# Count items' one-hots by one comparison with a scalar per partition and item, in place of packed two-tensor comparisons over six items

## The reference, cut to what matters

```python
xl = (x @ W_l + b_l); xr = (x @ W_r + b_r); e = edge_attr @ W_e
g = leaky_relu(xl[src] + xr[dst] + e, 0.2)
logits = einsum('ehc,hc->eh', g, att)
alpha = softmax of logits over the edges of each dst
out = segment_sum(xl[src] * alpha[..., None], dst)
```

## Time and profile before

| | |
|---|---|
| median of 3 runs | 7927.81 us (7926.12 to 7949.97) |
| the profiled execution: time, span | 7968.06, 7966.3 us |
| TensorE busy, share of the span | 5155.2 us, 65% |
| GpSimd busy | 3868.2 us, 49% |
| VectorE busy | 3099.9 us, 39% |
| ScalarE busy | 1675.7 us, 21% |
| mean granted TensorE clock | 0.736 |

### The profile page before, as it was taken

The page is one execution under the profiler, slowest core; times in us unless marked ns, Lnnn a source line. Parts: engine busy times, 40 slices in busy tenths (PEclk is TensorE's granted clock), DMA queues, the critical chain, the costliest instruction groups (busy, mean ns, idle before and its releaser), DMA issues. The chain is left out here.

```text
span 7966.3 us, 113832 instructions
## 1 busy us (share of the span) xinstructions
PE 5155.2 (65%) x33329; PEld 4083.2 (51%) x33329; DVE 3099.9 (39%) x3830; ACT 1675.7 (21%) x3525; POOL 3868.2 (49%) x3496
## 2 busy tenths in 40 slices
PE   0106888888888884166598895666666666614656
PEld 0103555555555553166355555666666666614656
DVE  3427777777777774444301103111111111122101
ACT  0004455455545542034000000111111111100000
POOL 0246888888888886200000003777777777640000
PEclk9958889888888886577798895555555555557988
DMA  6114555555555553299597792444444444405665
GB/s 278 33 38 134 146 150 153 145 152 144 150 146 149 148 150 83 66 368 360 141 292 230 233 296 70 127 124 127 124 127 124 127 124 127 114 20 186 233 234 194
DMA packets 597834, 1268.50 MB, mean 159 GB/s; under 512 B 201373, under 2 KB 367006, under 8 KB 572008
## 3 DMA queue, kind: packets, MB, share of 16 engines
q1 hardware_dynamic: 319400, 734.86, 29.0%
q10 hardware_dynamic: 166656, 412.78, 15.1%
q0 software_dynamic: 111424, 117.64, 8.4%
HBM read 930.29 MB, written 491.91 MB: 179 GB/s over the span
## 5 line engine op out<-in xcount | busy, mean ns | idle before, releaser
L513 POOL DMA_INDIRECT att_gl<-tab_l,att_ix x1568 | 1960.6, 1250 | 487.4 <-issue 461.0
L944 POOL DMA_INDIRECT sum_gl<-tab_l,sum_ixs x1568 | 1554.3, 991 | 541.3 <-issue 499.6
L753 ACT ACTIVATE att_acc<-att_pc 128x392 bf16<-128x392 f32 x2352 | 1084.9, 496 | 1334.3 <-PE att_pc L532 1188.5
L909 PE MATMUL sum_pm<-sum_msg,sum_S 128*128 128x64 f32 x3136 | 717.2, 423 | 661.7 <-ACT sum_msg L921 661.7
L529 PE MATMUL att_pc<-att_ohl,att_ohv 128*128 128x392 bf16 x2352 | 856.0, 364 | 290.1 <-DVE att_ohl L628 290.0
L909 PEld LDWEIGHTS sum_pm<-sum_msg,sum_S 128*128 128x128 f32 x3136 | 683.5, 330 | 689.4 <-issue 679.5
L532 PE MATMUL att_pc<-att_acc,att_ohv 128*128 128x392 bf16 x2352 | 848.5, 361 | 163.5 <-ACT att_acc L753 159.7
L1620 PE MATMUL l_pn<-l_a,l_E 128*128 128x392 bf16 x4704 | 792.5, 332 | 78.2 <-DVE l_E L1533 68.8
L216 POOL MEMSET tab_hT<- 1x6272 f32 x2 | 10.6, 5318 | 1643.2 <-POOLq L206 1643.2
L886 DVE TENSOR_TENSOR sum_t<-sum_pb,sum_gl 128x512 f32<-128x512 f32 x196 | 135.5, 691 | 1699.9 <-DMA sum_gl<-tab_l,sum_ixs 1699.9
L897 PE MATMUL sum_pb<-sum_wbs,sum_ea 64*128 64x64 f32 x3136 | 694.5, 419 | 21.5 <-DMA sum_ea<-in_ea64T 21.5
(11 more groups left out here) (301 smaller groups left out, 5418.2 us busy)
## 6 DMA issues: line engine op xcount, KB each, us to landing
A<-att_acc SPq DMA_DIRECT2D x2352, 98.0 KB
l_a<-A SPq DMA_DIRECT2D x294, 784.0 KB, 4.3
l_at<-AT SPq DMA_DIRECT2D x98, 1568.0 KB
att_dall<-in_dst ACTq DMA_DIRECT2D x224, 448.0 KB
sum_dall<-in_dst SPq DMA_DIRECT2D x196, 512.0 KB, 5.0
tr_a<-A SPq DMA_DIRECT2D x49, 1568.0 KB, 11.7
AT<-tr_at ACTq DMA_DIRECT2D x49, 1568.0 KB, 12.0
tot<-att_o ACTq DMA_DIRECT2D x56, 1022.0 KB
```

What stands on the lines that cost most here:

```text
L513: nc.gpsimd.indirect_dma_start(out=gl[s][:, c, :], out_offset=None, in_=g.tab_l, in_offset=bass.IndirectOffsetOnAxis(ap=ix[s][:, c:c + 1], ...
L753: nc.scalar.activation(acc[c][m][:, :], pc[c][m % 2][:, 0:LO], ACT.Copy).then_inc(s_acc[c], 1)
L909: mm = nc.tensor.matmul(pm[s][:, j // SB, (j % SB) * W:(j % SB + 1) * W], S[s][:, j, :], msg[s][:, j, :], start=True, stop=True)
L944: nc.gpsimd.indirect_dma_start(out=gl[s][:, j, :], out_offset=None, in_=g.tab_l, in_offset=bass.IndirectOffsetOnAxis(ap=ixs[s][:, j:j + 1] ...
```

## The change

`items` makes, for each of the six items by itself, three tensor_scalar comparisons: the constant row of 128 numbers with rk, the same row with the kept flag, and the constant row of 392 with lo. The scalar is one 4-byte value per partition, taken from a column of `g.rk`, `g.keep` or `g.lo`. The doubled constants are single now, and the one-hots are stored one behind the other. TensorE waits item by item.

```diff
-        c_row2 = st.sb("c_row2", [P, P, 2], F16)
-        c_lo2 = st.sb("c_lo2", [P, LO, 2], F16)
+        c_row = st.sb("c_row", [P, P], F16)
+        c_lo = st.sb("c_lo", [P, LO], F16)
...
-        ohv = [[st.sb(f"ohv{c}_{h}", [P, CJ, P, 2], BF16) for h in range(2)] for c in range(CH)]
-        ohl = [[st.sb(f"ohl{c}_{h}", [P, CJ // 2, LO, 2], BF16) for h in range(2)] for c in range(CH)]
+        ohv = [[st.sb(f"ohv{c}_{h}", [P, CJ, 2, P], BF16) for h in range(2)] for c in range(CH)]
+        ohl = [[st.sb(f"ohl{c}_{h}", [P, CJ, LO], BF16) for h in range(2)] for c in range(CH)]
...
-                    if m == 0:
-                        pe.wait_ge(s_oh[c], i * (2 * CB) + (2 * t + 2))
+                    pe.wait_ge(s_oh[c], n + 1)
...
-                    nc.tensor.matmul(pc[c][m % 2][:, 0:LO], ohv[c][h][:, m, :, 0], ohl[c][h][:, m // 2, :, m % 2],
+                    nc.tensor.matmul(pc[c][m % 2][:, 0:LO], ohv[c][h][:, m, 0, :], ohl[c][h][:, m, :],
...
-                    v.tensor_tensor(ohv[c][h][:, :, :, :], spread(c_row2[:, :, :].unsqueeze(1), [P, CJ, P, 2]),
-                                    spread(g.vals[:, bass.ds(n0, CJ), :].unsqueeze(2), [P, CJ, P, 2]), ALU.is_equal)\
-                        .then_inc(s_oh[c], 1)
-                    v.tensor_tensor(ohl[c][h][:, :, :, :], spread(c_lo2[:, :, :].unsqueeze(1), [P, CJ // 2, LO, 2]),
-                                    spread(g.lo[:, bass.ds(n0, CJ)].rearrange("p (j two) -> p j two", two=2).unsqueeze(2),
-                                           [P, CJ // 2, LO, 2]), ALU.is_equal).then_inc(s_oh[c], 1)
+                    for m in range(CJ):
+                        for k, x in enumerate((g.rk, g.keep)):
+                            v.tensor_scalar(ohv[c][h][:, m, k, :], c_row[:, :], x[:, bass.ds(n0 + m, 1)], None, ALU.is_equal)
+                        v.tensor_scalar(ohl[c][h][:, m, :], c_lo[:, :], g.lo[:, bass.ds(n0 + m, 1)], None, ALU.is_equal)\
+                            .then_inc(s_oh[c], 1)
...
-    g.vals = st0.sb("vals", [P, NI, 2], F16)
-    g.lo = st0.sb("lo", [P, NI], F16)
+    g.rk = st0.sb("rk", [P, NI])
+    g.keep = st0.sb("keep", [P, NI])
+    g.lo = st0.sb("lo", [P, NI])
```

More of the change, by code:

```diff
@@ L440, in _ @@
                     dve.wait_ge(s_io, 1)
-                    for k in range(2):
-                        nc.vector.tensor_copy(c_lo2[:, :, k], c_lo_i[:, :]).then_inc(s_one, 1)
-                        nc.vector.tensor_copy(c_row2[:, :, k], g.count[:, :]).then_inc(s_one, 1)
+                    nc.vector.tensor_copy(c_lo[:, :], c_lo_i[:, :]).then_inc(s_one, 1)
+                    nc.vector.tensor_copy(c_row[:, :], g.count[:, :]).then_inc(s_one, 1)
                     dve.wait_ge(s_k, 1)
@@ L524, in item @@
                     h = t % 2
-                    if m == 0:
-                        pe.wait_ge(s_oh[c], i * (2 * CB) + (2 * t + 2))
+                    pe.wait_ge(s_oh[c], n + 1)
                     if not known(n, 2):
                         pe.wait_ge(s_acc[c], n + (-1))
-                    nc.tensor.matmul(pc[c][m % 2][:, 0:LO], ohv[c][h][:, m, :, 0], ohl[c][h][:, m // 2, :, m % 2],
+                    nc.tensor.matmul(pc[c][m % 2][:, 0:LO], ohv[c][h][:, m, 0, :], ohl[c][h][:, m, :],
                                      start=True, stop=False)
                     wait_reuse(pe, s_acc[c], n)
-                    nc.tensor.matmul(pc[c][m % 2][:, 0:LO], ohv[c][h][:, m, :, 1], acc[c][(m - 1) % CR][:, :],
+                    nc.tensor.matmul(pc[c][m % 2][:, 0:LO], ohv[c][h][:, m, 1, :], acc[c][(m - 1) % CR][:, :],
                                      start=False, stop=True).then_inc(s_mm[c], 1)
@@ L1380, in _ @@
                 step(v.tensor_scalar(rkr[:, :, :], rkr[:, :, :], -1.0, 255.0, ALU.max, ALU.min))
-                for k, to in enumerate((g.vals[:, :, 0], g.lo[:, :])):
+                for k, to in enumerate((g.rk[:, :], g.lo[:, :])):
                     for n, r in enumerate(range(0, IT, 4)):
@@ L1393, in _ @@
                 step(v.tensor_scalar(near[:, :], near[:, :], g.dcol1[:, :], -1.0, ALU.mult, ALU.add))
-                step(v.tensor_copy(g.vals[:, :, 1], near[:, 0:NI]))
+                step(v.tensor_copy(g.keep[:, :], near[:, 0:NI]))
                 dve.sem_inc(s_e, 1)
```

## The result

The changed kernel takes 8114.74 us (median of 4 runs, 8105.52 to 8118.13), the kernel before beside it 7932.11 us (4 runs). The ratio is 1.0225, with a 95% interval from 1.0205 to 1.0244: slower by 2.2%, 11 us above the forecast of 8104. The profiled execution took 8118.1 us.

The account below looks back on a forecast made before the run. GpSimd's gathers were taken to bound the edge loop; afterwards VectorE's 1011 + 1298 + 170 us plus 150 of waits give 2629 against 2453, +176 on 7968, less 40: 8104 us; whole range 7700 to 8430.

Parts of the forecast that it names:

- The one-hots' price: VectorE's comparisons in the edge loop: 552 ns an item, 1298 us in all, 449 more than before.
- the hidden scalar: Rival: on VectorE the scalar's read hides behind the instruction in front; about 7725 us, chance 0.26.
- no doubling: Rival: 16-bit data doesn't double VectorE's rate for these comparisons, 1698 us of one-hots; about 8445 us, chance 0.13.
- The Trainium skill's faster tier for a tensor_scalar: On VectorE a 16-bit tensor_scalar may reach 4x: about 350 ns an item, one-hots level with before.
- The collision term: In the edge loop gathers hold up VectorE's comparisons: 0.2 us for some 850 of 1568 gathers, +170 us.
- nothing completes ... about 0.25 us less one interval: Among VectorE's comparisons, none completes from about 0.75 us of a gather to 0.05 us behind its 0.94.
- The remaining waits: VectorE's waits for TensorE and ScalarE in the edge loop: 150 us kept of 356.
- The bound changed sides: In the edge loop VectorE, with 2479 us to do, becomes the bound; GpSimd's floor is 2130 us.
- The loop ends when GpSimd has issued its gathers: In the edge loop before the change GpSimd is occupied for 99% of 2453 us and sets its end.
- The forecast's own range: Whole kernel, with collisions from 0 to 310 us and waits from 60 to 300 us: 7960 to 8330 us.
- TensorE's finer wait: TensorE in the edge loop waits per item instead of per six; counted as no cost.
- the lock between VectorE and GpSimd: Rival: GpSimd keeps VectorE's comparisons out for a whole gather; about 9850 us, chance 0.03.

Follow-up runs that it names:

- kernel 2: The changed kernel with the constant 1.0 in place of each comparison's scalar per partition: 7961.18 us, ratio 0.9989 to the kernel before.
- kernels 9 and 11: 9: the changed kernel with TensorE waiting once per six items, ratio 1.0997; 11: the changed kernel unaltered on the same slower chip, ratio 1.0828.
- kernel 12: The changed kernel with rows and keeps packed for six items again, columns still item by item: 7895.86 us, ratio 0.9915 to the kernel before.
- kernel 4: The kernel before with one gather in seven, the other rows constant: 7935.77 us, ratio 0.9960 to the kernel before.

## Why the prediction was right

- **The one-hots' price held.** 0.16, 0.16 and 0.23 us from start to start were forecast and measured; 1298 us forecast, 1311 by the medians. The three parts hold one by one: 0.26 ns a column, and 58 ns for the scalar (60 in kernel 2), unhidden. This refutes the two rivals that held most of the other chance, the hidden scalar and no doubling. Kernel 2 also shows that the first was priced too low: without the scalar the gathers go back to 1260 ns, which its 7725 us left out.
- **The Trainium skill's faster tier for a tensor_scalar** (VectorE: DVE Perf Modes, "The perf-mode tier table") fits the slope: 0.26 ns a column is half of the packed comparison's 0.52. Without the scalar's cost, which the page doesn't give, its estimate was an even result. Kernel 2 comes out even, 0.9989, but not for that reason alone: its one-hots take 909 us, not the page's 823 (350 ns an item), and GpSimd is full again.
- **The collision term was mis-sized:** 170 us forecast, 28 to 45 measured. The step that failed is "nothing completes ... about 0.25 us less one interval": completion is held up, the next start hardly.
- **The remaining waits were mis-sized too:** 150 us forecast, 292 measured. Of these 26 x 3.55 = 92 us are the pauses after branches, which no step of the prediction has. They could have been read: ScalarE, with 323 instructions a turn in the trace, pauses 3.2 us (median) after the branches in the kernel before. The two errors (142 too many, 142 too few) cancel, and the loop's 2629 us against 2631 owe their closeness to that. It is luck, and so is a good part of the 11 us by which the forecast missed.
- **The bound changed sides, as said:** VectorE is 89% busy, GpSimd waits 490 us for messages, gathers take 1047 ns, TensorE waits 419 us.
- **"The loop ends when GpSimd has issued its gathers" was only just true.** With one gather in seven the kernel before gains 50 us. GpSimd's 99% hid a chain through TensorE, ScalarE and VectorE nearly as long.
- **The forecast's own range doesn't follow from its terms.** Collisions from 0 to 310 and waits from 60 to 300 us give a loop of 2369 to 2919 us, so 7844 to 8394 and not 7960 to 8330. The result lies in both.
- **TensorE's finer wait isn't nothing** (kernels 9 and 11). The prediction took its effect as nothing in either direction. It may have a part in kernel 12's gain too, which shorter gathers alone don't explain.
- The loop accounts for 179 us of the profiles' difference of 150. The 29 us the other way lie behind the loop, which the change doesn't touch; the profiled execution of before was also 36 us above its median. The medians lie 183 us apart.

## What to carry to other kernels

Price a scalar per partition at some 60 ns an instruction on VectorE, and add it to the instruction's own 70 ns (0.102 us from start to start for 33 ns of columns, kernel 2) before splitting a packed operation: at 392 columns the faster column rate nearly repaid both (0.231 us against 1.30 / 6 = 0.217), at 128 it didn't (0.162 against 0.87 / 12 = 0.073). An engine that is 99% occupied may still bind the loop by little: take its work away in a trial before pricing what freeing it gives (here 50 us, kernel 4). Shortening the two-input VectorE instructions that hold up transfers' issues went with a gain in kernel 12, beside other differences. Count the instructions in a loop body when unrolling, and look for an engine that already pauses at its branch.

## What the runs showed of the hardware beside that

- An engine's pause after a loop branch depends on its body (instructions a turn in the trace, medians): VectorE 0.26 to 0.29 us at 198 and 3.2 to 3.7 us at 338, 394, 399, 506 and 646; ScalarE 2.5 to 3.3 us at 323; SyncE 1.4 to 3.9 us at 464; GpSimd 0.22 us at 74. TensorE pauses 0.05 to 0.2 us though its weight loads and register instructions alone are 518 to 629, so length alone isn't the rule for every engine.
- Comparisons with a constant make gathers 1260 ns long, the same with a scalar per partition 1047. That a gather gets in while the scalar is fetched would explain it, but no run shows it.
- On two of the chips SyncE and VectorE go through stretches in which each instruction takes 0.70 us or more, one that only sets a register too; the kernel before then takes 9195 and 9373 us instead of 7932 to 7966.
- Of the lock between VectorE and GpSimd that the Trainium skill states for a whole instruction (SBUF — State Buffer, "Who interferes with whom"), the changed kernel shows a hold of at most 0.2 us on a comparison (432 against 243 ns, 461 against 311) and 12 ns an item on the starts behind it.
